# First attention keeps its output transposed and goes through DRAM; the orders of all engines written anew

## The reference

```python
x = x + _L0_xattn_ref(_layernorm(x), ctx, ctx, Wq, Wk, Wv, Wo)   # 32 query heads, 8 KV heads, width 16
x = x + _L0_ffn_ref(_layernorm(x), weight, bias, lora_A, lora_B, starts)
x = x + _L1_xattn_ref(_layernorm(x), ctx, ctx, Wq, bq, Wk, bk, Wv, bv, 16)   # softmax over batch and head
x = x + _L1_ffn_ref(_layernorm(x), W_base, b_base, enc0, enc1, coefs0, coefs1, mask0, mask1)
```

## Time and profile before

| | |
|---|---|
| median of the runs | 297.38 us (297.06 to 297.87) |
| the profiled execution | 297.65 us, its span 295.9 us |
| PE busy | 290.2 us, 98% |
| DVE busy | 232.1 us, 78% |
| ACT busy | 162.2 us, 55% |
| POOL busy | 146.9 us, 50% |
| DMA | 33.10 MB, mean 112 GB/s |

### The profile page before, as it was taken

One profiled execution on the slowest core, in us unless ns is written; L12 is line 12 of the kernel. 1 busy time (PEld: TensorE's weight loads), 2 busy tenths in 40 slices (PEclk: granted clock), 3 DMA queues, 4 the chain that ended last, 5 costly groups with the idle time before them and its releaser, 6 DMA issues.

```text
span 295.9 us, 6338 instructions
## 1 busy us (share of the span) xinstructions
PE 290.2 (98%) x2192; PEld 229.8 (78%) x2192; DVE 232.1 (78%) x374; ACT 162.2 (55%) x276; POOL 146.9 (50%) x193
## 2 busy tenths in 40 slices
PE   6999999999999999999999999999999999999996
PEld 2788776856875675688998998898996778888885
DVE  5689787798968975366594966889978799989772
ACT  5957767873388257744437256463745367443220
POOL 6784304270338031225130285386388849998451
PEclk9999999999999999999999999999999999999999
DMA  7956376318034421001433142441444612000112
GB/s 252 351 155 232 112 231 221 107 40 311 31 126 145 142 73 41 0 2 31 139 106 95 52 141 52 125 116 45 128 150 111 210 42 69 2 3 35 73 71 106
DMA packets 32137, 33.10 MB, mean 112 GB/s; under 512 B 3609, under 2 KB 21273, under 8 KB 32107
## 3 DMA queue, kind: packets, MB, share of 16 engines
q1 hardware_dynamic: 32106, 32.70, 35.4%
HBM read 18.39 MB, written 2.10 MB: 69 GB/s over the span
## 4 chain that ended last, share of the span: by engine, by line
PE 91%; POOL 4%; DVE 1%; issue 1%; ACT 1%; POOLq 0%; ACTq 0%; DVEq 0%
PE ps L490 18%; PE ps L492 17%; PE ps L491 17%; PE ps L755 5%; PE ps L665 5%; PE ps L835 4%; PE ps L722 3%; PE ps L744 3%; PE ps L763 3%; PE ps L874 3%; PE ps L847 2%; PE ps L772 1%; PE ps L885 1%; PE ps L919 1%; PE ps L678 1%
## 5 line engine op out<-in xcount | busy, mean ns | idle before, releaser
L1225 DVE TENSOR_REDUCE mx<-ps 128x8 f32<-128x1024 f32 x32 | 37.9, 1218 | 4.2 <-PE ps L722 4.0
L1438 POOL TENSOR_SCALAR var_eps<-moments 128x1 f32<-128x1 f32 x32 | 7.1, 222 | 67.9 <-DVE moments L1187 67.0
L1426 POOL TENSOR_TENSOR slot_l<-stg,slot_h 128x512 fp32r<-128x512 f32 x19 | 26.1, 1386 | 21.9 <-ACT slot_h L943 21.9
L490 PE MATMUL ps<-xT_h,slot_h 128*128 128x256 f32 x128 | 36.9, 289 | 0.0
L1022 ACT ACTIVATE PT<-ps 128x1024 f32<-128x1024 f32 x32 | 31.7, 1023 | 8.8 <-PE ps L744 8.7
L492 PE MATMUL ps<-xT_h,slot_l 128*128 128x256 f32 x128 | 36.0, 281 | 0.0
L491 PE MATMUL ps<-xT_l,slot_h 128*128 128x256 f32 x128 | 36.0, 281 | 0.0
L490 PEld LDWEIGHTS ps<-xT_h,slot_h 128*128 128x128 f32 x128 | 24.2, 189 | 2.0 <-issue 0.6
L1468 POOL TENSOR_TENSOR zpart<-P 128x512 f32<-128x512 f32 x16 | 21.3, 1330 | 7.2 <-ACT P L1089 6.3
L491 PEld LDWEIGHTS ps<-xT_l,slot_h 128*128 128x128 f32 x128 | 24.2, 189 | 0.3
L492 PEld LDWEIGHTS ps<-xT_h,slot_l 128*128 128x128 f32 x128 | 24.2, 189 | 0.0
...
## 6 DMA issues: line engine op xcount, KB each, us to landing
ctx_in<-in_ctx SPq DMA_DIRECT2D x20, 256.0 KB, 3.4
QS<-Q_h SPq DMA_DIRECT2D x16, 256.0 KB, 2.9
...
X<-in_x SPq DMA_DIRECT2D x8, 256.0 KB, 4.3
stg<-in_wq SPq DMA_DIRECT2D x8, 256.0 KB, 4.1
QS<-Q_l SPq DMA_DIRECT2D x8, 256.0 KB, 3.0
out<-XB SPq DMA_DIRECT2D x7, 256.0 KB, 2.0
KS<-K_h SPq DMA_DIRECT2D x8, 128.0 KB, 2.4
```

The lines of the kernel that those rows point to most:

```text
L490: eng.matmul(dst, left[0], right[0], start=start, stop=False)
L1225: dve.tensor_reduce(mx[:, b % 2, :].rearrange("p (x r) -> p r x", r=REP)[:, r, :], wide(step).rearrange("p k (g t) -> p (k g) t", g=4), AX ...
L1426: pool.tensor_tensor(lo, src, hi.bitcast(F32), ALU.subtract).then_inc(w_lo_pool, 1)
```

## The change

Steps OB are gone. The output stays as PV leaves it, with the 16 values of a head on partitions. For each b, SP writes the two halves of OTs to a DRAM scratch `o_dram` (OW.b.0, OW.b.1, 256 KB each) and reads the 8 x 16 value rows back, packed to 128 partitions, into O (OR.b, 256 KB). It also copies the eight rows of sums within SBUF to 32 partitions of `zin` (ZR.b, 16 KB). PE transposes them (ZT.b, one product), DVE inverts them into rec, ACT spreads them 16-fold into z_wide (ZE.b), PE transposes this (ZB.b, four products), and DVE multiplies O by it. OX.b is now only the split of O by ACT and DVE. The rows of Wo are loaded in the matching order. ACT's copy of PV.(b+1) waits until OW.b and ZR.b have landed; OR.b waits until OX.(b-1) has read O. POOL fills `zin` in SET.0. Some small tiles of the norms get fewer buffers, and the five orders are new.

```diff
-LX.0 LX.1 LC.0.0 LW.wkv.0 LI LW.wkv.1 LC.0.1 LW.wq0.0 LW.wq0.1 LW.wq0.2 LX.2 LW.wq0.3 LC.0.2 LX.3 LX.5 LC.0.3 LX.4
...
-LC.0.6 QL.3 LW.w0.3 LW.w0.2 LW.lb.0 LW.w0.0 DM.3 LW.wk1.1 QL.5 QL.4 LC.1.0 LC.1.1 KL.2 DM.4 LW.wk1.2 LW.w0.1 KL.3
-DM.5 QL.6 LW.wq1.0 QL.7 LC.1.2 DM.6 LW.wq1.1 LW.wk1.3 DM.7 LW.wk1.0 LW.wq1.2 LW.wq1.3 LC.1.3 QX.1 QX.0 QX.3 LW.wv1.3
...
+LC.0.4 LX.5 LW.wo.3 KL.0 QL.0 DM.0 LW.wo.0 QL.1 LX.6 LC.0.5 LW.wo.1 LW.w0.3 KL.1 LC.0.7 LX.7 DM.1 LW.wo.2 ZR.0
+OW.0.0 OW.0.1 QL.2 LC.0.6 OR.0 DM.2 LS OW.1.0 ZR.1 OW.1.1 QL.3 OR.1 LW.w0.0 LW.w0.2 DM.3 QL.4 ZR.2 OW.2.1 OW.2.0
+LC.1.0 OR.2 KL.2 LW.la.0 OW.3.0 LC.1.1 ZR.3 OW.3.1 LW.w0.1 OR.3 DM.4 LW.lb.0 LW.wk1.2 QL.5 LW.wk1.0 DM.5 QL.6 OW.4.0
+OW.4.1 ZR.4 KL.3 OR.4 OW.5.1 OW.5.0 DM.6 ZR.5 LW.wk1.1 QL.7 DM.7 OR.5 LW.wk1.3 OW.6.0 OW.6.1 ZR.6 LW.wq1.3 LC.1.2
+OR.6 OW.7.1 ZR.7 OW.7.0 LW.wq1.0 OR.7 LE LW.wq1.2 LW.wq1.1 LC.1.3 QX.1 QX.0 LW.wv1.1 QX.2 LW.wv1.0 QX.3 QX.5 QX.4
+LW.wv1.2 LC.1.4 LC.1.5 QX.7 QX.6 LC.1.6 LC.1.7 LW.wv1.3 LL QX.9 QX.8 QX.11 QX.10 LW.dft.1 LW.dft.0 LW.dft.2 LC.2.4
...
-XT.0.1:4 XT.0.0:7 V0.0:0 V0.1:1 Q0.0.0:5 K0.0:0 Q0.0.1:6 MX.0.1:4 MX.0.0:0 V0.2:3 MX.0.3:6 MX.0.2:4 XT.0.3:2 V0.3:3
...
-F0.1:2 MT.6:0 MX.7.1:4 MX.7.3:6 PV.5.0:0 OX.4:2 F0.0:3 OB.5.1:2 ST.6.1:0 ST.6.2:6 ST.6.3:4 WO.4:3 OB.5.0:1 MT.7:0
-XT.1.3:2 ST.6.0:4 OX.5:0 PV.6.1:7 PV.6.0:2 ST.7.3:5 OB.6.1:3 OB.6.0:0 XT.1.2:1 ST.7.0:2 ST.7.2:6 ST.7.1:4 WO.5:0
-OX.6:6 PV.7.1:2 PV.7.0:3 OB.7.1:2 XT.2.1:6 OB.7.0:5 WO.6:4 OX.7:7 K1.1:3 LT.1:2 XT.2.0:6 WO.7:1 F0.3:6 Q1.1:7 Q1.0:3
...
+XT.0.0:3 XT.0.1:0 V0.1:2 V0.0:7 Q0.0.0:3 K0.0:7 Q0.0.1:4 MX.0.1:0 MX.0.0:2 V0.2:6 XT.0.3:7 MX.0.2:0 MX.0.3:4 V0.3:6
...
+MX.5.0:4 K0.3:6 Q0.3.1:0 MT.4:6 ZT.3:1 MX.5.1:4 MX.5.2:2 WO.2:7 ZB.3:2 XT.1.1:4 MX.6.3:5 ST.4.0:0 MT.5:2 Q0.3.0:3
+ST.4.3:0 ST.4.1:4 ST.4.2:6 WO.3:2 XT.1.0:6 PV.4.0:3 MX.6.0:0 ST.5.1:4 MX.6.1:6 PV.4.1:2 ST.5.2:0 ST.5.3:4 MX.6.2:2
+LT.0:6 MX.7.1:0 ST.5.0:2 PV.5.1:4 MT.6:5 ZT.4:7 PV.5.0:1 MX.7.2:4 MX.7.0:6 MX.7.3:2 F0.0:1 ZB.4:4 MT.7:0 ST.6.2:6
+ZT.5:5 F0.1:3 ZB.5:1 ST.6.0:6 ST.6.3:4 ST.6.1:2 WO.4:0 PV.6.0:2 PV.6.1:7 ST.7.3:0 ST.7.2:4 ST.7.1:2 WO.5:7 ZT.6:0
+XT.1.2:2 ST.7.0:4 XT.1.3:1 ZB.6:7 PV.7.1:3 PV.7.0:4 XT.2.0:3 LT.1:2 WO.6:5 ZT.7:4 K1.0:0 ZB.7:6 F0.3:1 XT.2.1:7
+XT.1.5:4 WO.7:5 F0.2:6 XT.1.4:4 Q1.1:3 Q1.0:2 LT.2:5 Q1.3:7 K1.1:1 F0.4:3 Q1.2:6 XT.2.2:2 S1.0:4 S1.1:0 K1.2:7
...
+SET.8 LNn.0.0 W.wkv.0 XT.0.0 W.wkv.1 XT.0.1 W.wq0.0 W.wq0.1 W.wq0.2 V0.1 V0.0 W.wq0.3 K0.0 CT.0.2 Q0.0.0 CT.0.3
...
+ST.5.1 PV.4.1 ST.5.2 ST.5.3 LT.0 ST.5.0 MT.6 PV.5.1 PV.5.0 ZE.4 ZE.5 OX.4 ST.6.2 MT.7 W.wk1.1 W.wk1.2 ST.6.0 ST.6.1
+ST.6.3 OX.5 PV.6.0 PV.6.1 ST.7.3 ST.7.2 ST.7.1 LNn.1.3 ZE.6 XT.1.2 ST.7.0 XT.1.3 PV.7.1 OX.6 PV.7.0 XT.2.0 LT.1
+W.wk1.3 ZE.7 LNn.1.5 OX.7 BV XT.1.5 XT.2.1 K1.0 W.wq1.3 W.wq1.0 W.wq1.1 LNn.1.4 C0 XT.1.4 Q1.1 W.wq1.2 LNn.2.3 Q1.0
...
-SET.1 SET.2 SET.0 LNs.0.0 LNs.0.1 L.wkv.1 L.wq0.0 L.wq0.2 L.wq0.3 KM.0 LNs.0.2 LNs.0.3 CL.0.3 KM.1 LNs.0.4 L.wo.2
...
+SET.2 SET.0 SET.1 LNs.0.0 LNs.0.1 L.wkv.1 L.wq0.0 L.wq0.2 L.wq0.3 KM.0 LNs.0.3 CL.0.3 LNs.0.2 KM.1 LNs.0.4 LNs.0.5
...
-        stats = sb("stats", [4, B, 6])
-        moments = sb("moments", [4, B, 2])
-        var_eps = sb("var_eps", [4, B])
-        rstd = sb("rstd", [4, B])
-        shift = sb("shift", [4, B])
+        stats = sb("stats", [4, 6])
+        moments = sb("moments", [2, B, 2])
+        var_eps = sb("var_eps", [4])
+        rstd = sb("rstd", [2, B])
+        shift = sb("shift", [2, B])
...
-            rec = s1("rec", [2, REP, 4])
+            zin = s1("zin", [P])
+            rec = s1("rec", [REP, KVH])
+            z_wide = s1("z_wide", [REP, KVH, HD0])
...
+        o_dram = nc.dram_tensor("o_dram", (B, KVH, 2 * HD0, D), F32, kind="Internal").ap()
...
+                    if name == "wo":
+                        src = w.rearrange("(g r d) n -> r g d n", g=KVH, r=REP)[c]
...
-                    sp.dma_start(KS[0:P:HALF, :, :, :, :].bitcast(F32), ones[:, :]).then_inc(one_loaded, 16)
+                    sp.dma_start(KS[0:P:HALF, :, :, :, :].bitcast(F32), rec[:, :, :]).then_inc(one_loaded, 16)
+                elif kind == "OW":
+                    b, gq = step[1:]
+                    consumed(sp, ("PV", b, gq))
+                    sp.dma_start(o_dram[b, 4 * gq:4 * gq + 4, :, :].rearrange("j x n -> (j x) n"),
+                                 OTs[:, gq, :]).then_inc(o_written, 16)
+                elif kind == "OR":
+                    b = step[1]
+                    sp.wait_ge(o_written, 16 * 2 * (b + 1))
+                    if b:
+                        sp.wait_ge(ot_ready, OT_PARTS[("OX", b - 1)] + 1)
+                    sp.dma_start(O[:, :], o_dram[b, :, 0:HD0, :]).then_inc(u_loaded, 16)
+                elif kind == "ZR":
+                    b = step[1]
+                    consumed(sp, ("PV", b, 0))
+                    consumed(sp, ("PV", b, 1))
+                    sp.wait_ge(zin_set, 1)
+                    if b:
+                        filled(sp, ("ZT", b - 1))
+                    sp.dma_start(zin[0:KVH * REP, :], OTs[HD0:P:2 * HD0, :, :]).then_inc(z_loaded, 16)
...
-                elif kind == "OB":
-                    b, gq = step[1:]
-                    dst = take(pe, step)
-                    consumed(pe, ("PV", b, gq))
+                elif kind == "ZT":
+                    b = step[1]
+                    dst = take(pe, step)
+                    pe.wait_ge(z_loaded, 16 * (b + 1))
+                    pe.transpose(dst[:, 0:P], zin[:, :], ident[:, :]).then_inc(psum_full, 1)
+                elif kind == "ZB":
+                    b = step[1]
+                    dst = take(pe, step)
+                    pe.wait_ge(wide_ready, b + 1)
                     for r in range(REP):
-                        last = pe.transpose(dst[:, r * P:(r + 1) * P], OTs[:, gq, r * P:(r + 1) * P],
+                        last = pe.transpose(dst[:, r * P:(r + 1) * P], z_wide[:, r, :, :].rearrange("p g d -> p (g d)"),
                                             ident[:, :])
                     last.then_inc(psum_full, 1)
-                elif kind == "OX":
-                    b = step[1]
-                    dst = take(pe, step)
-                    consumed(pe, ("OB", b, 0))
-                    consumed(pe, ("OB", b, 1))
-                    for c in range(C):
-                        last = pe.transpose(dst[:, c * P:(c + 1) * P], O[:, c * P:(c + 1) * P],
-                                            ident[:, :])
-                    last.then_inc(psum_full, 1)
                 elif kind == "WO":
                     b = step[1]
                     dst = take(pe, step)
-                    consumed(pe, ("OX", b))
+                    pe.wait_ge(ot_ready, OT_PARTS[("OX", b)] + 1)
...
+                elif kind == "ZE":
+                    b = step[1]
+                    consumed(act, ("ZT", b))
+                    if b:
+                        filled(act, ("ZB", b - 1))
+                    act.activation(z_wide[:, :, :, :], rec[:, :, :].unsqueeze(3).broadcast_to([P, REP, KVH, HD0]),
+                                   ACT.Copy).then_inc(wide_ready, 1)
                 elif kind == "PV":
                     b, gq = step[1:]
                     filled(act, step)
                     if b:
-                        filled(act, ("OB", b - 1, gq))
+                        act.wait_ge(o_written, 16 * 2 * b)
+                        act.wait_ge(z_loaded, 16 * b)
                     act.activation(OTs[:, gq, :], place(step), ACT.Copy).then_inc(act_freed, 1)
                 elif kind == "OX":
                     b = step[1]
-                    filled(act, step)
+                    consumed(act, ("ZB", b))
                     if b:
                         filled(act, ("WO", b - 1))
-                    act.activation(OT_h[:, :, :], place(step).rearrange("p (c t) -> p c t", c=C),
+                    act.activation(OT_h[:, :, :], O[:, :].rearrange("p (c t) -> p c t", c=C),
...
-                elif kind in ("XT", "OX"):
+                elif kind == "OX":
                     hi_written(dve, step)
-                    if kind == "OX":
-                        lo, hi = [t[:, :, :] for t in (OT_l, OT_h)]
-                    else:
-                        ts = (fT_l, fT_h) if step[1] == 1 else (xT_l, xT_h)
-                        lo, hi = [t[:, :, step[2] % 2, :] for t in ts]
+                    dve.tensor_tensor(OT_l[:, :, :], O[:, :].rearrange("p (c t) -> p c t", c=C), OT_h[:, :, :].bitcast(F32),
+                                      ALU.subtract).then_inc(ot_ready, 1)
+                elif kind == "XT":
+                    hi_written(dve, step)
+                    ts = (fT_l, fT_h) if step[1] == 1 else (xT_l, xT_h)
+                    lo, hi = [t[:, :, step[2] % 2, :] for t in ts]
...
-                elif kind == "OB":
-                    b, gq = step[1:]
+                elif kind == "ZT":
+                    b = step[1]
                     filled(dve, step)
                     if b:
```

(49 more changed lines are left out.)

119 lines of the change are left out of this document (55 added, 64 removed).

## The result

The changed kernel takes 301.44 us (median of 4 runs, 300.69 to 303.18) against 297.35 of the kernel before (297.06 to 297.87) in the same comparison: a ratio of 1.0144, 95% interval 1.0098 to 1.0190. Run again later, unaltered, it gave 300.33 against 297.63, 1.0091 (1.0059 to 1.0124). The second run had been expected to repeat the 1.014. It is slower by about 1%. The forecast was 293.5 us, range 291.4 to 296.2, with 0.88 on faster. It missed by 8 us.

What follows compares the result with a forecast made beforehand. The prediction took PE to bound the kernel (busy 98% of the span, 91% of the chain of waits). 297.65 - 6.0 + 1.7 + 0.4 = 293.75, less 0.27 for the median, gave 293.5 us, range 291.4 to 296.2.

Steps and rivals of the forecast that it cites:

- OB gone, ZT come: PE's work: 7.2 us of OB transposes removed, 1.2 us of ZT transposes added; net -6.0 us, between -5.1 and -7.0.
- POOL's start: Kernel start: SET.2 and SET.0 ahead of SET.1 delay PE to 3.9 and the first transpose to 8.8; +1.7 us.
- OW, "0.55 + 2.0": Round trip of the values: 0.55 us for SP to issue the write OW, 2.0 us from issue to landing.
- OR, "and then 2.9": Round trip of the values: the packed read OR lands 2.9 us after its issue.
- OR "behind two other loads of SP in the order": Round trip of the values: OR's issue comes behind two other loads in SP's order; whole trip some 9 us against 9.2.
- What stands behind its new waits ... is needed 3 us or more after it is issued.: SP's order: KL.3 behind ZR.4 and DM.6 behind OW.5.0 are needed 3 us or more after issue.
- Stalls of all round trips: PE's waits for all eight round trips of sums and values: +0.4 us, bounds 0 to 2.5.
- The orders' new places: Other steps moved in the orders: priced at nothing, -1 to +1 us, since PE takes the same number one after another.
- DVE 3.3 us lighter: DVE's work: loses 10.8 us of inversions and multiplications, gains 7.5; 3.3 us lighter, hidden by PE.
- the round trips come late: Rival, chance 0.07: ZR lands late for ZT at each b; 300.2 us if landing takes 4.5 us, so slower than before.
- The later start is not paid: Rival, chance 0.12: the clock rises sooner in the unread products or POOL's fills overlap; 1.7 us less, 291.8 us.
- the other: Rival, chance 0.09: DVE sets the pace between 60 and 80 us, so only its 3.3 us relief shows; 296.2 us.

Runs made afterwards that it cites:

- e5: Changed kernel without the packed read OR and its waits on SP and DVE; DVE's product takes X[:, b, :] instead; 295.82 us.
- e2: Changed kernel with OR reading the 16 depths of a head outermost and the 8 heads inside, spread sums and Wo rows to match; 297.33 us.
- e8: Kernel before with only POOL's first three steps in the changed kernel's order (SET.2 SET.0 SET.1); 298.86 us against 297.96.
- e3: Changed kernel with POOL's old start order (SET.1 SET.2 SET.0) put back and the packed read OR on 16 queues; 295.53 us.

## Why the prediction was wrong

The sum of the forecast was -6.0 + 1.7 + 0.4 = -3.9. The unaltered second run has a profile without the dip of the clock (300.33 us, +2.7 on 297.65), and divides so: first XT 9.18 against 7.14, +2.0; PE's waits 8.9 against 1.3, +7.6; what is left over, taken as PE's own work, -7.0. The 7.6 divide by e5 and e2: 3.2 without any read, 2.1 more with a read on sixteen queues, 2.3 more on eight. The ratios of the same three kernels put the last two at 1.5 and 3.1 us.

- **OB gone, ZT come: -6.0, bounds -5.1 to -7.0.** Within its bounds, at the far end: -7.0, as a remainder of the division above and not measured by itself. PE's busy time is 287.6 us (286.2 in the second run), not the 284 to 285 that were named as the sign.
- **POOL's start: +1.7.** Right in kind and nearly in size. PE's first product at 3.91 (3.9 forecast), first XT at 9.19 (8.8). The 0.4 between are in the unread products: the forecast took over their 4.85 us, but in the kernel before the last one already starts 0.68 behind the one ahead of it, and here all six stand 0.85 to 1.0 apart. The forecast held that each microsecond of it counts in full. In the kernel before it doesn't: 1.55 us of the first XT cost 0.9 in e8. Between e2 and e3 2.38 us are worth 1.8, but their intervals leave 1.0 to 2.6.
- **ZR and ZT.** Right: ZR lands in 1.9 to 2.4 us, once 3.9 (three times 3.1 to 3.6 in the second run), with 2.0 taken, and ZT waits for nothing in the second run.
- **OW, "0.55 + 2.0".** The median of 2.2 bears it out, the spread was not allowed for: up to 4.0. At b = 6, where it counts, it took 4.0 in one execution and 2.3 in the other, and PE's idle time before LT.1 was 1.96 and 0.51. Why it varies is open.
- **OR, "and then 2.9".** This step failed. 2.9 is the row of the copies QS<-Q_h, from SBUF to SBUF; the load of the same size from DRAM has 3.4 in the same. Measured were 4.1 to 5.3 (5.6 in the second run). The packing that makes its slowest dimension 8 halves the queues, and on sixteen the median is 3.7. With 3.7 (e2) the kernel is no slower than before, 0.9986.
- **OR "behind two other loads of SP in the order".** This failed too. The issue was priced by SP's order alone, and the wait for OX.(b-1), which there is because O is a single tile, at nothing. From the end of ACT's copy to the product the forecast has about 6.5 us; measured are 13.9 at b = 5, 11.5 at b = 3 and 8.2 at b = 6. A second tile for O was not tried, so how much of the loss is the late issue and how much the landing is known only for the landing's part (e2).
- **"What stands behind its new waits ... is needed 3 us or more after it is issued."** This was asked of SP alone, and failed there too: DM.4 stood behind OR.3, which waits for OX.2, and its copy of the maxima then took 4.6 us (2.0 to 3.1 for the others). Of DVE it was not asked at all, and that is the main failure. DVE waits in its order for OR ahead of additions and halves that PE's banks need, so the question "is the product in time for WO?" (9.0 against 9.2) was the wrong one. This is where most of the 4.4 us that e5 takes away came from; 0.8 of them are PE's wait for DM.4.
- **Stalls of all round trips: +0.4, bounds 0 to 2.5.** Too small by far; 4.4 even where only the read is counted.
- **The orders' new places: 0, -1 to +1.** Probably too low for the first layer: 3.2 us more of waits than before stay with no read, and what causes them was not separated. In the second layer the steps' distances add up to the same as before.
- **DVE 3.3 us lighter.** It became 0.2 lighter (231.9). The inversions take 0.35, not 0.25, and DVE's half of OT grew from 0.686 to 1.013 in the mean, +2.6 (below).
- **OW by the formula, 2.6 us.** The Trainium skill (DMA: Bandwidth & Descriptors, "Anatomy of one DMA") gives the 2.0 us plus bytes over 436 GB/s for DMAs that GpSimd issues; here SyncE issues all. The median of the writes, 2.2, stays under the 2.6 that the prediction works out from it; the longest, 4.0, does not.

Of the rivals, "the round trips come late" had the sign right, and its price, 300.2, is near the 301.4, but by luck: it was priced for ZT, which was in time. "The later start is not paid" is true in part (e8), and the other fell: DVE is no busier where PE waits (16.96 of 20 us between 60 and 80, from 18.79); it stands.
